# Gate and up of 1024 tokens by seven block products, with the weight sums made during attention

## What is computed

```python
q = (x @ Wq.T + bq).reshape(B, S, H, D)          # 16 heads of 32; k and v alike
q = _apply_rope(q, cos, sin)
k = _apply_rope(k, cos, sin)
qk = jnp.einsum('bshd,bstd->bsht', q, k) / jnp.sqrt(jnp.float32(D))
att = jax.nn.softmax(qk, axis=-1)                # over the 16 heads of a token
out = jnp.einsum('bsht,bstd->bshd', att, v)
...
x = _layernorm(x + out @ Wo.T + bo)
g = jnp.einsum('th,ih->ti', xf, gate_w) * gate_s # INTER = 1408 rows
u = jnp.einsum('th,ih->ti', xf, up_w) * up_s
hdn = jax.nn.silu(g) * u
x = _layernorm(x + jnp.einsum('ti,hi->th', hdn, down_w) * down_s)
```

## Time and profile before

| | us |
|---|---|
| median of 3 runs | 1918.01 |
| lowest and highest of the runs | 1915.58 and 1918.29 |
| the profiled execution: its own time | 1914.57 |
| the profiled execution: span from the first to the last instruction | 1912.8 |
| PE busy in the span | 1833.2 (96%) |
| DVE busy | 1185.1 (62%) |
| POOL busy | 740.3 (39%) |
| ACT busy | 713.4 (37%) |

### The profile page before, as it was taken

One profiled execution on the slowest core, in us unless ns is written; L12 is line 12 of the kernel. 1 busy time (PEld: TensorE's weight loads), 2 busy tenths in 40 slices (PEclk: granted clock), 3 DMA queues, 4 the chain that ended last, 5 costly groups with the idle time before them and its releaser, 6 DMA issues.

```text
span 1912.8 us, 41015 instructions
## 1 busy us (share of the span) xinstructions
PE 1833.2 (96%) x15490; PEld 1480.8 (77%) x15490; DVE 1185.1 (62%) x1734; ACT 713.4 (37%) x1138; POOL 740.3 (39%) x571
## 2 busy tenths in 40 slices
PE   6899999999999999994999999999999999999997
PEld 5777888888878888883788888888888888888885
DVE  6678898888998888985244444444444444434443
ACT  4435555455554455543222222222222222222221
POOL 5767787777777777871011011100111011100111
PEclk8899999999999999997999999999999999999998
DMA  6355555665556655575511111102111111101101
GB/s 197 85 144 144 152 138 156 168 164 139 150 140 164 168 145 153 139 203 139 204 39 48 52 56 44 66 33 66 38 60 44 54 57 42 66 33 66 38 28 44
DMA packets 257790, 194.47 MB, mean 102 GB/s; under 512 B 143056, under 2 KB 182608, under 8 KB 257744
## 3 DMA queue, kind: packets, MB, share of 16 engines
q1 hardware_dynamic: 257744, 193.84, 36.4%
HBM read 109.13 MB, written 84.67 MB: 101 GB/s over the span
## 4 chain that ended last, share of the span: by engine, by line
PE 42%; issue 9%; POOL 1%; DVE 0%; DMA 0%; ACT 0%; POOLq 0%; DVEq 0%; SPq 0%; ACTq 0%
PE ps_g L833 7%; PE ps_g L830 7%; PE ps_u L830 7%; PE ps_u L833 7%; PE acc L850 7%; PE acc L847 7%; POOL z L913 1%; DMA dscale<-down_s 0%; DVE xT_lo L982 0%; DVE z L962 0%; POOL rs L915 0%; POOLq L702 0%; DVE hid L930 0%; ACT act_g L880 0%; DVE z L944 0%
## 5 line engine op out<-in xcount | busy, mean ns | idle before, releaser
L930 DVE SCALAR_TENSOR_TENSOR hid<-ps_u,gu_scale,act_g 128x512 f32<-128x512 f32 x176 | 132.1, 751 | 451.3 <-ACT act_g L880 451.3
L913 POOL TENSOR_TENSOR z<-z,wide 128x512 f32<-128x512 f32 x64 | 80.6, 1289 | 731.1 <-DVE z L944 731.1
L880 ACT ACTIVATE act_g<-ps_g,gu_scale 128x512 f32<-128x512 f32 x176 | 121.3, 689 | 574.9 <-PE ps_u L833 574.9
L325 PE MATMUL ps_x<-w_hi,xc_hi 128*128 128x512 f32 x768 | 310.2, 404 | 17.5 <-POOL xc_lo L483 7.9
L326 PE MATMUL ps_x<-w_lo,xc_hi 128*128 128x512 f32 x768 | 306.7, 399 | 0.0
L329 PE MATMUL ps_x<-w_hi,xc_lo 128*128 128x512 f32 x768 | 306.4, 399 | 0.0
L504 POOL TENSOR_TENSOR qk_cos<-qk_in,rot 128x512 f32<-128x512 f32 x128 | 203.8, 1592 | 170.0 <-DVE qk_in L575 145.6
L847 PE MATMUL acc<-wf_rest,hid_hi 128*128 128x512 f32 x640 | 252.6, 395 | 1.2 <-DVE hid_lo L936 1.2
L833 PE MATMUL ps_g<-xT_lo,wf_rest 128*128 128x512 f32 x640 | 253.2, 396 | 0.0
L850 PE MATMUL acc<-wf_rest,hid_lo 128*128 128x512 f32 x640 | 252.8, 395 | 0.0
L830 PE MATMUL ps_u<-xT_hi,wf_rest 128*128 128x512 f32 x640 | 252.6, 395 | 0.0
(11 more groups left out here) (87 smaller groups left out, 2955.1 us busy)
## 6 DMA issues: line engine op xcount, KB each, us to landing
xc<-x_cols SPq DMA_DIRECT2D x32, 512.0 KB, 4.7
v_rows<-v_in SPq DMA_DIRECT2D x32, 512.0 KB, 4.1
v<-v_rows SPq DMA_DIRECT2D x32, 512.0 KB, 5.4
res<-x_rows SPq DMA_DIRECT2D x64, 256.0 KB, 3.2
x_rows<-x_out SPq DMA_DIRECT2D x32, 512.0 KB, 4.0
x_cols<-x_turn SPq DMA_DIRECT2D x128, 128.0 KB, 2.4
wide<-x_rows SPq DMA_DIRECT2D x16, 1024.0 KB, 5.6
out<-z SPq DMA_DIRECT2D x64, 256.0 KB, 3.1
```

Source lines behind the costliest of these rows:

```text
L325: pe.matmul(out, hi[:, k], w_hi[:, w, k], start=(k == 0), stop=False)
L930: dve.scalar_tensor_tensor(out=hid[:, :], in0=slot(u, j)[1][:, :], scalar=gu_scale[:, 1, j:j + 1], in1=act_g[:, :], op0=ALU.mult, op1=ALU. ...
```

## The change

Gate and up of a chunk are 256 rows of output by 512 of inner size, cut into 2 x 2 blocks of weights, and 1024 tokens instead of 512 are taken at a time, so that x has 2 x 2 blocks too (two halves of the tokens, two of the inner size). Strassen's algorithm in Winograd's form gives the four output blocks by seven products of blocks in place of eight.

- **FFN, PE.** A super is 1024 tokens; there are 8. Per chunk `product` runs 7 times, each 2 pieces x 2 (x_hi, x_lo) = 4 matmuls, with four banks (`ORDER`): products 5, 6 and 7 add onto a bank that products 1, 3 and 4 have left and that must first have been read. Then come the 8 matmuls `down1` of the first 512 tokens for the chunk before. There are only eight banks, so the down product of the other 512 tokens (`down2`) waits until all chunks are through, and then runs as 10 x 8 matmuls in a row plus 8 before the last `down1`; the hidden values `hid2` are kept in SBUF till then.
- **FFN, the other engines.** Outputs are put together from sums of banks. DVE has 8 operations per chunk, ACT 4 or 5. In the `down2` stretch ACT makes the high parts `h2_hi` and the high parts of the next super's seven x operands, POOL the low parts `h2_lo` (two buffers each), and DVE the low parts of the x operands. Four sums of x blocks are made by POOL during the chunks.
- **FFN, DMA.** The seven weight operands are no longer all in SBUF. They are streamed again for every super, 0.92 MB per chunk, through three slots.
- **Attention.** Each unit now makes 1/32 of the weight operands: 4 sums of 88 columns on POOL, then high and low parts of 9 x 88 = 792 columns, in place of 528. High and low part move from lag 1 to lag 2, `f_abs` from lag 2 to lag 3, and `f_lo` stands near the start of POOL's step and no longer at its end. So that the parts of a weight lie side by side, ACT first copies all weights from DRAM to DRAM (`relay`, 11 chunks in the first five steps).

```diff
+                if (m := unit_of(s, 2, UNITS)) is not None:
+                    sp.wait_ge(f_lo_done, m + 1)
+                    for dn, gu, half, stored in ((dn_hi, gu_hi, f_hi, f_hi_stored), (dn_lo, gu_lo, f_lo, f_lo_stored)):
+                        sp.dma_start(dn[:, bass.ds(m * 2 * PART, 2 * PART)],
+                                     half[:, 0:2].rearrange("p o c -> p (o c)").bitcast(F32)).then_inc(stored, 16)
+                        sp.dma_start(gu[:, :, bass.ds(m * PART, PART)].rearrange("o p c -> p o c"),
+                                     half[:, 2:9].bitcast(F32)).then_inc(stored, 16)
                 if (m := unit_of(s, 1, UNITS)) is not None:
                     at_least(sp, f_lo_done, m)
-                    sp.dma_start(f_raw[:, :], ffn_w[m]).then_inc(f_loaded, 16)
-                if (m := unit_of(s, 2, UNITS)) is not None:
-                    sp.wait_ge(f_lo_done, m + 1)
-                    sp.dma_start(ffn_hi[m], f_hi[:, :].bitcast(F32)).then_inc(f_hi_stored, 16)
-                    sp.dma_start(ffn_lo[m], f_lo[:, :].bitcast(F32)).then_inc(f_lo_stored, 16)
+                    batch = s - 1 if isinstance(s, int) and s < LAGS else LAGS - 1
+                    sp.wait_ge(relaid[batch], 16 * relay_parts[batch])
+                    sp.dma_start(f_all[:, 1:3].rearrange("p o c -> p (o c)"), dn_raw[:, bass.ds(m * 2 * PART, 2 * PART)])\
+                      .then_inc(f_loaded, 16)
+                    sp.dma_start(f_all[:, 0], gu_raw[0, :, bass.ds(m * PART, PART)]).then_inc(f_loaded, 16)
+                    sp.dma_start(f_all[:, 3:6], gu_raw[1:4, :, bass.ds(m * PART, PART)].rearrange("o p c -> p o c"))\
+                      .then_inc(f_loaded, 16)
...
+            def relay(s, j):
+
+                for dst, src, lo, hi in chunk_parts(j):
+                    act.dma_start(dn_raw[:, lo:hi] if dst is None else gu_raw[dst, :, lo:hi],
+                                  ffn_w[src // SLAB, :, src % SLAB:src % SLAB + hi - lo]).then_inc(relaid[s], 16)
...
+                if (m := unit_of(s, 2, UNITS)) is not None:
+                    act.wait_ge(f_summed, 4 * m + 4)
+                    at_least(act, f_hi_stored, 2 * 16 * m)
+                    at_least(act, f_lo_done, m)
+                    act.activation(f_hi[:, :, :], f_all[:, 1:10], ACT.Copy).then_inc(f_hi_done, 1)
...
-                if (m := unit_of(s, 2, UNITS)) is not None:
+                if (m := unit_of(s, 3, UNITS)) is not None:
...
                                    accum_out=lo_top[:, bass.ds(m, 1)]).then_inc(lo_seen, 1)
...
                 if (m := unit_of(s, 1, UNITS)) is not None:
-                    act.wait_ge(f_loaded, 16 * (m + 1))
-                    at_least(act, f_hi_stored, 16 * m)
-                    at_least(act, f_lo_done, m)
-                    act.activation(f_hi[:, :], f_raw[:, :], ACT.Copy).then_inc(f_hi_done, 1)
...
+                if (m := unit_of(s, 2, UNITS)) is not None:
+                    pool.wait_ge(f_hi_done, m + 1)
+                    at_least(pool, f_lo_stored, 2 * 16 * m)
+                    at_least(pool, lo_seen, m)
+                    pool.tensor_tensor(f_lo[:, :, :], f_all[:, 1:10], f_hi[:, :, :].bitcast(F32), ALU.subtract)\
+                        .then_inc(f_lo_done, 1)
...
-                    pool.wait_ge(f_hi_done, m + 1)
-                    at_least(pool, f_lo_stored, 16 * m)
-                    at_least(pool, lo_seen, m)
-                    pool.tensor_tensor(f_lo[:, :], f_raw[:, :], f_hi[:, :].bitcast(F32), ALU.subtract)\
-                        .then_inc(f_lo_done, 1)
+                    pool.wait_ge(f_loaded, 3 * 16 * (m + 1))
+                    at_least(pool, f_hi_done, m)
+                    at_least(pool, f_lo_done, m)
+                    a21, a22, a12, a11 = (f_all[:, o] for o in (0, 3, 4, 5))
+                    s1, s2, s3, s4 = (f_all[:, o] for o in (6, 7, 8, 9))
+                    pool.tensor_tensor(s1, a21, a22, ALU.add).then_inc(f_summed, 1)
+                    pool.tensor_tensor(s3, a11, a21, ALU.subtract).then_inc(f_summed, 1)
+                    pool.wait_ge(f_summed, 4 * m + 1)
+                    pool.tensor_tensor(s2, s1, a11, ALU.subtract).then_inc(f_summed, 1)
+                    pool.wait_ge(f_summed, 4 * m + 3)
+                    pool.tensor_tensor(s4, a12, s2, ALU.subtract).then_inc(f_summed, 1)
...
+        A22, A12, A11, S1, S2, S3, S4 = range(OPS)
+        ORDER = ((A11, bank_a), (S2, bank_b), (S3, bank_d), (S1, bank_e), (A12, bank_a), (A22, bank_d), (S4, bank_e))
+        FIRST = 4
...
+                def product(n, j, i):
+                    w, out = ORDER[i]
...
+                        pe.wait_ge(xhi_done, OPS * n + i + 1)
+                        pe.wait_ge(xlo_done, OPS * n + i + 1)
+                    if i < FIRST and j == 0:
+                        at_least(pe, z_read[1], T4 * (n - 1) + i + 1)
+                    elif i < FIRST:
+                        pe.wait_ge((silu1_done, u2_done, c21_done, c12_done)[i], c)
+                    else:
+                        pe.wait_ge((s1_done, u3_done, c22_done)[i - FIRST], c + 1)
+                    for k in range(KH):
+                        cols = slice(k * P, k * P + P)
+                        start, stop = i < FIRST and k == 0, k == KH - 1
+                        pe.matmul(out[:, :], slot[:, w, cols], x_hi[:, i, k], start=start, stop=False,
+                                  skip_group_check=True)
...
+                        last = pe.matmul(out[:, :], slot[:, w, cols], x_lo[:, i, k], start=False, stop=stop,
+                                         skip_group_check=True)
+                    last.then_inc(prod_done, 1)
...
                     for j in range(NJ):
-                        if tile_of(i, u, 1, BLOCKS):
-                            gate_up(i, u, j)
-                        if j == 0 and tile_of(i, u, 2, BLOCKS):
-                            down(i, u, 2, NJ - 1)
-                        if j > 0 and tile_of(i, u, 1, BLOCKS):
-                            down(i, u, 1, j - 1)
...
+                        for i in range(OPS):
+                            product(n, j, i)
+                        if j > 0:
+                            down1(n, j - 1)
+                    down2(n, 0)
+                    down1(n, NJ - 1)
+                    for j in range(1, NJ):
+                        down2(n, j)
...
+            def high_of_hid2(n, j):
+                act.wait_ge(hid2_done, NJ * n + j + 1)
+                if j == 0:
+                    at_least(act, rows2_done, T4 * n)
+                else:
+                    at_least(act, down2_done, (NJ - 1) * n + j - 1)
+                act.activation(h2_hi[:, j % 2], hid2[:, j], ACT.Copy).then_inc(h2hi_done, 1)
...
+                    if j == NJ - 1:
+                        high_of_hid2(n, 0)
+                        high_of_hid2(n, 1)
+                    chunk(n, j)
+                for j in range(2, NJ):
+                    high_of_hid2(n, j)
+                    if next_ is not None and j - 2 < OPS:
+                        high_of_x(next_, j - 2)
...
+            def chunk(n, j):
+                c, done = NJ * n + j, OPS * NJ * n + OPS * j
+                dve.wait_ge(prod_done, done + 2)
+                dve.wait_ge(s1_done, c + 1)
+                at_least(dve, c12_done, c)
+                dve.tensor_tensor(u2[:, :], bank_b[:, :], s1[:, :], ALU.add).then_inc(u2_done, 1)
+                dve.wait_ge(prod_done, done + 3)
+                dve.wait_ge(u2_done, c + 1)
+                at_least(dve, c22_done, c)
+                dve.tensor_tensor(u3[:, :], bank_d[:, :], u2[:, :], ALU.add).then_inc(u3_done, 1)
+                dve.wait_ge(prod_done, done + 4)
+                dve.wait_ge(u3_done, c + 1)
+                at_least(dve, h2lo_done, c + 1 - NJ)
+                dve.tensor_tensor(hid2[:, j], bank_e[:, :], u3[:, :], ALU.add).then_inc(c22_done, 1)
+                dve.wait_ge(prod_done, done + 6)
+                at_least(dve, h1lo_done, c)
+                dve.tensor_tensor(hid1[:, :], bank_d[:, :], u2[:, :], ALU.add).then_inc(c21_done, 1)
+                dve.wait_ge(c21_done, c + 1)
+                dve.wait_ge(silu1_done, c + 1)
+                dve.scalar_tensor_tensor(out=hid1[:, :], in0=hid1[:, :], scalar=gu_scale[:, 1, j:j + 1], in1=sg1[:, :],
+                                         op0=ALU.mult, op1=ALU.mult).then_inc(hid1_done, 1)
+                dve.wait_ge(prod_done, done + 7)
+                at_least(dve, hid2_done, c)
+                dve.tensor_tensor(sg2[:, :], bank_e[:, :], u2[:, :], ALU.add).then_inc(c12_done, 1)
+                dve.wait_ge(h1hi_done, c + 1)
+                dve.tensor_tensor(h1_lo[:, j % 2], hid1[:, :], h1_hi[:, j % 2].bitcast(F32), ALU.subtract)\
+                   .then_inc(h1lo_done, 1)
+                dve.wait_ge(c22_done, c + 1)
+                dve.wait_ge(silu2_done, c + 1)
+                if j in (1, 4):
```

(13 more changed lines are left out.)

592 lines of the change are left out of this document (355 added, 237 removed).

## The result

| | kernel before | changed kernel |
|---|---|---|
| median of the runs | 1917.4 us (1915.6 to 1918.3) | 1984.6 us (1974.9 to 1986.1) |
| ratio | | 1.034 (95% interval 1.031 to 1.038) |
| the profiled execution | 1914.6, span 1912.8 | 1985.2, span 1983.4 |
| first to last matmul of the FFN | 986.25 for 4224 matmuls | 995.74 for 3872 |
| unit of attention | 26.28 | 27.3 |

What follows compares the result with a forecast made beforehand. PE was taken to bound both attention and FFN. The terms -82 + 35 + 10 + 1 + 25 + 32 + 5 + 5 = +31, added to a median of 1918, gave 1949 us, slower, in a range of 1890 to 1990.

Steps and rivals of the forecast that it cites:

- start of attention: Attention's first steps: ACT issues weight copies, at 0.43 us each, before its spread of k; +10 us (+2 to +25).
- 352 matmuls fewer: FFN on PE: 28 matmuls in place of 32 per chunk of 1024 tokens, 0.2335 us each; -82.2 us.
- ring of attention: Attention: exponential, f_abs, f_lo, rotations in a row make the unit 27.5 for 26.28 us; +35 us (0 to +43).
- drain and FFN start: Drain of attention, +1 us; FFN start, DVE's sums and low parts delay PE, +5 us.
- chunk stalls: FFN chunks: DVE's statistics and POOL's adds and sums delay products; +25 us (0 to +45).
- down2 stretch: FFN's down2 matmuls: two buffers, and h2_lo waiting for DVE's operations, make PE wait; +32 us (+13 to +55).
- end: End of the FFN: statistics and pow ahead of POOL's adds, normalise beside them; +5 us.
- rival 4: Much slower: idle time in attention units lowers PE's clock, POOL's sums and locks at upper ends; 1998 us, chance 0.18.
- rivals 2 and 3: 2: FFN clean, attention's ring binds, 1912 us, chance 0.08; 3: faster on both, 1877 us, chance 0.10.
- Rival 1: Attention's ring does not bind, FFN as in the forecast; 1914 us, chance 0.11.

Runs made afterwards that it cites:

- e1: Changed kernel with ACT's f_abs of the unit before moved to the front of its attention step: 1950.4 us.
- e2: Changed kernel with weights laid out by the host, without ACT's DRAM copies and the waits for them: 1966.4 us.
- e5: Changed kernel with four buffers instead of two for hid2's high and low parts in the down products: 1961.9 us.
- e3: Changed kernel with VectorE's FFN loop over super-blocks written out, without a branch: 1973.1 us.
- e10: Changed kernel with POOL's four sums moved, one each in chunks 6 to 9, started by u2 (VectorE's first sum of the chunk): 1962.5 us.
- e6: Changed kernel with VectorE's FFN work in smaller portions, and POOL's adds and sums spread, started at product 1 of a chunk: 1980.1 us.
- e8: Kernel with the edits of e1, e2, e3, e5 and e6, but POOL starts adds and sums at VectorE's first sum (u2), not product 1: 1860.3 us.
- e11: e8 with VectorE's residual-row adds moved to the next super-block's chunks, and POOL's first hid2 low part waiting for u2 of chunk 10: 1854.0 us.
- the five edits: The edits of e1, e2, e3, e5 and e6, each on the changed kernel; all together in one kernel: 1905.0 us.

## Why the loss was twice the forecast

The sign and the range held, and every term that the prediction named came up, but their sum was 31 where the spans show 70.6. Two steps failed. The chunks of the FFN were to lose 25, by statistics, adds and sums alone, with a PE at full clock and a VectorE that goes from one super-block to the next without loss; they lost 66, of which 13.9 were VectorE's branch and 14.3 the half clock behind the waits. And the start of attention was to cost 10, by issues of 0.43 us; it cost 20. The terms for the ring and the stretch were 6 too high each and hid 12 of the error, which is luck. By the prediction's own terms, on the spans (1912.8 to 1983.4):

| term | forecast | measured | by |
|---|---|---|---|
| 352 matmuls fewer | -82.2 | -82.2 | 3872 at 0.2335 as the floor |
| ring of attention | +35 | +28.6 | 28 x 1.02; e1 |
| start of attention | +10 | +20.3 | the ninth load is 25.4 late, less 5 units of 1.02; e2 |
| drain and FFN start | +6 | +5.3 | from the last load of x to the first FFN matmul 104.4 for 99.1 |
| chunk stalls | +25 | +66 | the chunks without the stretches |
| down2 stretch | +32 | +26 | 25.71 for 22.42; e5 |
| end | +5 | +6.9 | 20.5 for 13.6 from the start of the last matmul |
| sum | +31 | +70.9 | 70.6 by the spans; the floor is rounded |

**Ring: right, in place, mechanism and size.** The unit was to be 27.5 and is 27.3. One sign of it was wrong: VectorE's idle time before `top` was to be gone, and 0.8 us of it is still there.

**Start: the mechanism right, the term mis-sized by two.** The step that failed is "SP's issue of a DMA takes 0.43", used for ACT's queue. There it is 0.64, and 31 copies, not 29, stand before the first spread of k: 20 us, not 12.5. The 23 in step 4, taken as hidden in part, stop ACT a second time for 13.

**Chunk stalls: the step that failed most, in three ways.** What it named and took as 25 was 31: the sums 15.2 (2.2 per super-block, where I took 2.0), the statistics 11.3 + 1.6 (1.8 per super-block where I took 1.0; in chunk 1 VectorE is late from chunk 0 already), and 3.0 in chunk 3, behind POOL's adds and the normalising, where I took 0.6 per super-block. What it did not name was DVE's branch, 13.9. And the half clock, 16.6 with the 2.3 at the FFN's start, stood in rival 4 alone, tied to attention and to 2.5 us of idle time; it came in the FFN, behind waits of 1.94 us and more. With some 4 for matmuls that start a little later behind a wait these make 66. e3 and e10 take out the branch and the sums, one each, and the half clock falls to 7.2 and 7.5 with either. The statistics have no run of their own: e6 split them and lost the gain to POOL's marks, and only in e8, with all edits, do chunk 1's waits fall to 6.4.

**Down2 stretch: size nearly right, by luck, since the cause was wrong.** I had 1.6 of its 4.3 from the two buffers, and the rest from `h2_lo` held up by DVE's low parts of x. It is the other way round: the last super-block has no low parts of x beside its stretch and takes 25.2 all the same, so that the two buffers cost 2.8 and the low parts 0.5. In the stretch

```profile
1197.48 1.54 POOL L1116 TENSOR_TENSOR h_lo<-hid,h_hi 128x512 fp32r<-128x512 f32 x1 [0.69 <-ACT h_hi L1048]
...
1199.79 1.48 POOL L1116 TENSOR_TENSOR h_lo<-hid,h_hi 128x512 fp32r<-128x512 f32 x1 [0.76 <-ACT h_hi L1048]
1200.03 4.55 DVE L1161 TENSOR_TENSOR x_lo<-wide,x_hi 128x1024 fp32r<-128x1024 f32 x2
```

POOL's operation takes 1.5 for 1.29, while DVE's take 2.3 for 1.22: DVE bears the lock. The step is 2.23 apart in place of 1.87 because of the chain of free buffer, ACT and POOL, and e5 removed the wait with two more buffers and nothing done about locks.

**The clean FFN of rivals 2 and 3** had the right idea of what could be had (e11's FFN is 15 us above the floor of its matmuls, where this one is 92), but not in the order of work that this change has. Rival 1 fell with the unit of 27.3; rival 4 named 1998 and the half clock, but from attention, where it did not appear: the granted clock of the window at 600 us is 1.00.

Two sums of the prediction are off without weight: 986 - 82 + 5 + 57 is 966 and not 963 for the FFN, and a unit moves 0.3 MB more than before (4.35 for 4.05), not half a megabyte.

**What stays open.** How much of the half clock is due to which wait: it fell behind some waits of 1.94 to 3.3 us and not behind others of the same length, and never behind a shorter one than 1.9 in the twelve profiles with this FFN (e3 has seven waits of 1.94 in chunk 1 and none of them is followed by it). How the 22 us of the copies divide among ACT's issues, traffic and landing is open too. Also not tried was a smaller number of copies at the start, or their issue by another engine.

## What to carry to other kernels

When work is taken from the bounding engine and given to two others that share a port, count the room of each and then look at which operations overlap: one wait with the right mark was worth 45 us here, more than any other single edit. Start helper work on GpSimd at the moment at which VectorE begins to read PSUM, not when PE has got somewhere: VectorE's four operations that read PSUM take 0.69 each with or without POOL beside them. And after each stall removed, look for the one that it hid: the five edits gave 34, 18, 12, 23 and 4 us one by one, 91 in sum, and only 80 together; with the right mark it was 124. In the traces the three in the FFN shorten it by 12.4, 19.6 and 3.7, together by 24.6, and with the right mark by 71.0.

## What was not expected of the hardware

- The branch of VectorE's loop in the FFN costs the engine some 3 us before its next instruction (4.0 to 4.5 idle, 1.2 or less without a branch), each of the five times round. The branch of its loop in attention leaves 0.8 of idle time at most. Why the two differ no run here shows.
- VectorE's `tensor_scalar` on fp32 tiles in SBUF, one input, locks with GpSimd too: 1.91 alone, 3.99 and 3.87 beside it. The Trainium skill (SBUF — State Buffer, Who interferes with whom) names this form among those that take both ports in their fast mode; the runs agree, and I had counted only operations with two inputs.
- In these profiles the lock falls on the one that comes second: DVE's 0.75 became 2.93 beside a sum of 2.39 that had begun just before, and the next sum, begun 0.47 before this operation ended, took 2.74; DVE's 1.22 became 2.31 beside POOL's 1.29, which itself stayed at 1.5.
- ACT's issues of the copies took 0.64 us each; SP's issues of a unit in the same kernel lie between 0.33 and 0.65. An issue has no one price; the queue in question has to be looked at.
